# Two attention layers and two feed-forward layers on one core: the SwiGLU output transposed by DMA, expert programs written out, weight rounding in small pieces

## The reference

```python
x = x + attention_1(layernorm(x), ctx)      # 16 heads of 16, softmax
x = x + ffn_1(layernorm(x))                 # SwiGLU, 704 hidden columns, activations and weights rounded to 8 bits
x = x + attention_2(layernorm(x), ctx, ctx) # 4 heads of 64, gated (mLSTM), rms norm
x = x + experts(layernorm(x))               # 8 experts, the best 2 of each row
```

```python
logits = x @ gate_w;  weights, chosen = top_k(softmax(logits), 2);  weights /= weights.sum(-1)
for i in range(8):
    wi = where(chosen == i, weights, 0).sum(-1)
    h  = silu(x @ w1[i]) * (x @ w3[i])          # 256 -> 1024
    out += (h @ w2[i]) * wi
```

## Time and profile before

| | us |
|---|---|
| median of 3 runs | 826.21 (825.64 to 830.43) |
| the profiled execution | 830.6, its span 828.8 |
| attention 1, to the last `tail_add` | about 199 |
| first to last start of a tile's gate/up product, tiles 1 to 38 | 448.42 to 798.48 |
| PE busy | 677.7 (82%) |
| DVE busy | 505.0 (61%) |
| ACT busy | 417.8 (50%) |
| POOL busy | 253.9 (31%) |
| granted TensorE clock, mean | 0.893 |

### The profile page before, as it was taken

The page is one execution under the profiler, slowest core; times in us unless marked ns, Lnnn a source line. Parts: engine busy times, 40 slices in busy tenths (PEclk is TensorE's granted clock), DMA queues, the critical chain, the costliest instruction groups (busy, mean ns, idle before and its releaser), DMA issues.

```text
span 828.8 us, 18605 instructions
## 1 busy us (share of the span) xinstructions
PE 677.7 (82%) x4518; PEld 464.0 (56%) x4519; DVE 505.0 (61%) x1266; ACT 417.8 (50%) x927; POOL 253.9 (31%) x297
## 2 busy tenths in 40 slices
PE   2999999985866686577517999999999999999992
PEld 2788887764324334477413656566656656556661
DVE  5577779987597533688795464646455555464440
ACT  1466665555769335576324544645354545544420
POOL 3111111110245301544302253535344254353211
PEclk9799999997798897755558999999999999999996
DMA  9100000003000002311371525343432534612113
GB/s 271 34 13 13 13 13 13 7 1 102 1 0 0 1 15 108 124 37 32 102 256 27 161 45 132 77 134 76 115 88 34 170 85 124 182 28 32 32 14 114
DMA packets 45649, 58.46 MB, mean 71 GB/s; under 512 B 13296, under 2 KB 39216, under 8 KB 45072
## 3 DMA queue, kind: packets, MB, share of 16 engines
q1 hardware_dynamic: 38128, 47.79, 17.7%
q0 software_dynamic: 7488, 10.31, 7.8%
HBM read 145.90 MB, written 11.80 MB: 190 GB/s over the span
## 4 chain that ended last, share of the span: by engine, by line
PE 46%; DVE 19%; issue 17%; DMA 7%; ACT 3%; POOL 3%; DVEq 2%; ACTq 1%; POOLq 1%; SPq 0%
PE psum L991 14%; PE psum L1013 7%; DMA sum_dram<-region,row_token 5%; PE psum L705 3%; PE psum L689 3%; PE psum L712 3%; PE psum L1004 2%; PE psum L896 2%; PE psum L725 2%; PE psum L744 1%; PE psum L827 1%; PE psum L694 1%; DVE region L1366 1%; PE psum L886 1%; DVE region L1364 1%
## 5 line engine op out<-in xcount | busy, mean ns | idle before, releaser
L991 PE MATMUL psum<-region 128*128 x936 | 216.5, 381 | 15.0 <-issue 5.9
L991 PEld LDWEIGHTS psum<-region 128*128 128x128 bf16 x936 | 91.7, 98 | 116.6 <-issue 27.9
L633 POOL DMA_INDIRECT sum_dram<-region,row_token x39 | 62.1, 1593 | 198.1 <-DVE region L1870 196.0
L1013 PE MATMUL psum<-region 128*128 x936 | 110.2, 275 | 3.4 <-DVE region L1878 3.3
L1269 ACT ACTIVATE region<-psum 128x512 f32<-128x512 f32 x78 | 46.4, 595 | 113.7 <-PE psum L991 113.7
L1013 PEld LDWEIGHTS psum<-region 128*128 128x128 bf16 x936 | 91.5, 99 | 16.1 <-issue 5.1
L1853 DVE TENSOR_TENSOR region<-psum,region 128x512 f32<-128x512 f32 x78 | 54.0, 692 | 64.9 <-ACT region L1269 64.4
L1290 ACT ACTIVATE pause_a<-one_col 128x1 f32<-128x1 f32 x117 | 23.7, 202 | 77.9 <-issue 63.5
L526 POOL TENSOR_TENSOR region<-region,pair_mask 128x256 f32<-128x256 f32 x32 | 18.9, 612 | 137.9 <-ACT region L1058 137.9
L625 POOL DMA_INDIRECT region<-xrow_dram,row_token x39 | 40.9, 1048 | 59.6 <-DVE row_token L1848 27.2
L1878 DVE TENSOR_TENSOR region<-psum,region 128x1024 bf16<-128x1024 f32 x39 | 47.6, 1222 | 14.8 <-ACT region L1277 14.8
(11 more groups left out here) (297 smaller groups left out, 1294.9 us busy)
## 6 DMA issues: line engine op xcount, KB each, us to landing
region<-in_L_ffn_w SPq DMA_DIRECT2D x117, 1024.0 KB
region<-in_ctx SPq DMA_DIRECT2D x32, 128.0 KB, 2.5
region<-neg_max_dram SPq DMA_DIRECT2D x4, 1024.0 KB, 4.7
xrow_dram<-region SPq DMA_DIRECT2D x1, 2080.0 KB, 7.9
x_sb<-in_x SPq DMA_DIRECT2D x4, 512.0 KB, 6.6
region<-in_ctx SPq DMA_DIRECT2D x2, 1024.0 KB, 6.9
sum_dram<-x_sb SPq DMA_DIRECT2D x1, 2048.0 KB, 7.5
region<-in_L_ffn_w_down SPq DMA_DIRECT2D x1, 704.0 KB, 8.3
```

Source lines behind the costliest of these rows:

```text
L633: pool.indirect_dma_start(sum_dram, bass.IndirectOffsetOnAxis(ap=row_token[:, t:t + 1], axis=0), y_d[:, t % 2, :], None, compute_op=ALU.ad ...
L991: last = mm(psum[:, 2 * f + n, :], (xT_lo if xl else xT_hi)[:, p, k, :], weights_at(place, wl, n, k * F1 + f * FH, FH), start=(i == 0), st ...
L1013: last = mm(psum[:, 7, 0:D], (hT_lo if hl else hT_hi)[:, f, :], weights_at(place, wl, 2, f * D, D), start=(i == 0), stop=(i == 3 * (F1 // ...
```

## The change

1. **Expert stage, h.** PE's transposes of h are gone. Each half f of h is split before it is transposed: ACT copies 512 columns of `h_d` to bf16 as soon as the half is there, DVE makes the low half beside it (`h_pair`, 1024 bf16 columns), and SP issues one transposing DMA for each half (`transpose_h`, 128 x 1024 bf16, 256 KB). `down_d` waits for both transfers of its tile.
2. **Expert stage, order.** PE transposes x of tile t + 1 between the two halves of gate/up; ACT's and DVE's x split moves ahead with it. SP's step t is: the two transposing DMAs of tile t, then the loads of w3 for t + 4, w1 for t + 3 and w2 for t + 2.
3. **Programs.** PE's and SP's loops over tiles are written out; PE reads a tile's place once, in the middle of the second half of the tile before.
4. **Attention 1.** DVE's preparation of ffn 1 is cut into small pieces, in steps 2 to 15, and stands ahead of `tail_add` instead of behind it. POOL's and DVE's loops are written out; the power for the layer norm comes in three parts.

```diff
@@ PE, SP: one expert tile
-            def h_transposes(t, p):
-                pe.wait_ge(h_d_ready, 2 * t + 2)
-                for f in range(F1 // P):
-                    last = tr(bank(4, F1 // P, P, count=2)[:, f, :], h_d[:, p, f * P:(f + 1) * P], ident[:])
-                last.then_inc(th_done, 1)
-
-            def down_d(t, place, inner=False):
-                pe.wait_ge(hT_low, t + 1)
+            def down_d(t, place):
+                pe.wait_ge(hT_loaded, 32 * t + 32)
...
+                    half, c = divmod(f, FH // P)
+                    last = mm(psum[:, 7, 0:D], hT_d[:, t % 2, half, hl * (FH // P) + c, :], weights_at(place, wl, 2, f * D, D),
...
-                gate_up_half(t, p, 0, place, inner)
-                if inner or t >= 1:
-                    h_transposes(t - 1, 1 - p)
...
-                gate_up_half(t, p, 1, place, inner)
-                if inner or 0 < t < NT - 1:
-                    x_transposes(t + 1, 1 - p, loads_next, inner)
-                if inner or t >= 1:
-                    down_d(t - 1, place_of(t - 1), inner)
+                gate_up_half(t, p, 0, places[t])
+                if t < NT - 1:
+                    x_transposes(t + 1, 1 - p)
+                gate_up_half(t, p, 1, places[t])
+                if t >= 1:
+                    down_d(t - 1, places[t - 1])
...
+            def transpose_h(t, f):
+
+                sp.wait_ge(h_low_ready, 2 * t + f + 1)
+                if t >= 1 and f == 0:
+                    sp.wait_ge(hT_loaded, 32 * t)
+                if t >= 2 and f == 0:
+                    sp.wait_ge(dn_done, t - 1)
+                sp.dma_start_transpose(hT_d[:, t % 2, f, :, :], h_pair[:, t % 2, f, :]).then_inc(hT_loaded, 16)
...
-                if inner or t + 4 < NT:
-                    load_part(0, t + 4, p, inner)
-                    load_part(1, t + 4, p, inner)
-                if inner or t + 3 < NT:
-                    load_part(2, t + 3, 1 - p, inner)
...
+            for t in range(NT):
+                transpose_h(t, 0)
+                transpose_h(t, 1)
+                if t + 4 < NT:
+                    load_part(1, t + 4)
+                if t + 3 < NT:
+                    load_part(0, t + 3)
+                if t + 2 < NT:
+                    load_part(2, t + 2)
@@ ACT and DVE: one expert tile
-            def h_high(t):
-                act.wait_ge(th_done, t + 1)
-                act_fn(hT_hi, bank(4, F1 // P, P, count=2), ACT.Copy).then_inc(hT_high, 1)
+            def h_high(t, p, f, inner=False):
+                act.wait_ge(h_d_ready, 2 * t + f + 1)
...
+                act_fn(h_pair[:, p, f, 0:FH], h_d[:, p, f * FH:(f + 1) * FH], ACT.Copy).then_inc(h_high_ready, 1)
...
+            def h_low(t, p, f):
+                dve.wait_ge(h_high_ready, 2 * t + f + 1)
+                tt(h_pair[:, p, f, FH:2 * FH], h_d[:, p, f * FH:(f + 1) * FH], h_pair[:, p, f, 0:FH],
+                   ALU.subtract).then_inc(h_low_ready, 1)
@@ DVE: attention 1
-                if late:
-                    late()
+                for work in late:
+                    work()
+                if inner or b >= 1:
+                    tail_add(b - 1)
...
-            rest = (gate_up_maxima, weight_scales, down_rounded, gate_up_scaled, gate_up_shifted, gate_up_rounded, early_norms)
...
+            late[2] = [lambda: gate_up_maxima(0)]
+            late[3] = [lambda: gate_up_maxima(1)]
+            late[4] = [lambda: gate_up_maxima(2)]
+            late[5] = [down_maxima]
+            late[6] = [weight_scales, lambda: down_scaled_up(0)]
+            late[7] = [lambda: down_scaled_up(1), down_shifted]
+            late[8] = [down_rounded, lambda: gate_up_scaled(0, 1)]
+            late[9] = [lambda: gate_up_scaled(1, 5)]
+            late[10] = [lambda: gate_up_scaled(5, 8), lambda: x1_eps(0)]
+            late[11] = [lambda: gate_up_scaled(8, 12)]
+            late[12] = [lambda: gate_up_shifted(0), lambda: early_norms(0, 0, 2)]
+            late[13] = [lambda: gate_up_shifted(1), lambda: early_norms(0, 2, 4)]
+            late[14] = [lambda: x1_eps(1), gate_up_rounded]
+            late[15] = [lambda: early_norms(0, 4, 8), lambda: early_norms(1, B // 2, EARLY)]
```

More of the change, by code:

```diff
@@ L535, in _, with x1_rstd @@
             pool.wait_ge(consts_ready, 7)
[L536 to L540, removed]
-            for n, part in enumerate((slice(0, EARLY), slice(EARLY, B))):
+            def x1_rstd(n):
+                part = THIRDS[n]
                 pool.wait_ge(ln2_eps, n + 1)
                 nc.gpsimd.tensor_tensor(rstd[:, part], rstd[:, part], minus_half[:, part], ALU.pow).then_inc(rstd2_ready, 1)
+            for b in range(B):
+                mask_k(b, b % 2)
+                if b == EARLY:
+                    x1_rstd(0)
+            x1_rstd(1)
+            x1_rstd(2)
             def hidden_product(g, t):
@@ L993, in gate_up_half, with x_transposes @@
                 last.then_inc(gu_done, 1)
-            def x_transposes(t, p, loads, inner=False):
-                pe.wait_ge(xg_loaded[p], 16 * loads)
+            def x_transposes(t, p):
+                pe.wait_ge(xg_loaded[p], 16 * (t // 2) + 16)
                 for k in range(KT):
@@ L1324, in _ @@
             tile_step(NT - 1, 0, (NT - 1) // 2)
-            h_high(NT - 1)
         @block.vector
@@ L1396, in token_stats, with step @@
                 nc.vector.tensor_copy(mv[:, b, :], mv1[:]).then_inc(chain, 1)
-            def step(b, p, inner=False, late=None):
+            def step(b, p, inner=False, late=()):
                 softmax_shift(b, 0)
@@ L1457, in norm_x1, with early_norms @@
                                             ALU.subtract, ALU.mult).then_inc(x1n_step, 1)
-            def early_norms():
-                dve.wait_ge(rstd2_ready, 1)
-                norm_x1(range(EARLY))
+            def early_norms(n, first, end):
+                if first == THIRDS[n].start:
+                    dve.wait_ge(rstd2_ready, n + 1)
+                norm_x1(range(first, end))
             step(0, 0)
-            rest = (gate_up_maxima, weight_scales, down_rounded, gate_up_scaled, gate_up_shifted, gate_up_rounded, early_norms)
-            with dve.Fori(0, (B - 1 - len(rest)) // 2) as i:
-                step(2 * i + 1, 1, inner=True)
-                step(2 * i + 2, 0, inner=True)
-            for b in range(B - len(rest), B):
-                step(b, b % 2, late=rest[b - (B - len(rest))])
+            late = [[] for b in range(B)]
+            late[2] = [lambda: gate_up_maxima(0)]
[12 more added lines that the diff above has]
+            late[15] = [lambda: early_norms(0, 4, 8), lambda: early_norms(1, B // 2, EARLY)]
+            for b in range(1, B):
+                step(b, b % 2, late=late[b])
             tail_norm(B - 1)
@@ L1882, in tile_step @@
                 hidden_d(t, p, 0)
-                if inner or t >= 1:
-                    h_low(t - 1)
-                if not inner and t == 0:
-                    x_low(1, 1)
+                if inner or t < NT - 1:
+                    x_low(t + 1, 1 - p)
+                h_low(t, p, 0)
                 hidden_d(t, p, 1)
-                if inner or 0 < t < NT - 1:
-                    x_low(t + 1, 1 - p)
+                h_low(t, p, 1)
                 if inner or t + 2 < NT:
@@ L1909, in _ @@
             tile_step(NT - 1, 0, NT // 2 + 1)
-            h_low(NT - 1)
             weighted(NT - 1, 0)
```

137 lines of the change are left out of this document (68 added, 69 removed).

## The result

The changed kernel took 902.8 us (median of 4 runs, 902.4 to 903.7) against 827.4 for the one before: a ratio of 1.091, 95% interval 1.087 to 1.095. The forecast was 817, the range 801 to 845.

A forecast was written before the change was run, and what follows sets the result against it. PE's own work was taken to bound the expert stage and attention 1, except where something is late. Terms -35 - 11 + 40 + 4 - 7 = -9 us, from the median 826.2, gave 817 us; range 801 to 845, the forecast's own 806 to 824.

The forecast's parts named there:

- PE's tile, 8.2 us: Steady expert tile: without h's transposes and a second place read it falls from 9.16 to 8.2 us, -35 us in all.
- Together they have some 5 us of work in a tile of 8.2, so only where they stand in a chain matters: Expert stage, ACT and DVE: their copies and subtractions fit within a tile and matter only where a chain waits on them.
- The chain behind a half: End of a tile's second half to transfer issue: silu, product, high, low and issue take 3.1 us, leaving 5.1 for landing.
- The transfers: Transposing DMAs of h: 256 KB land in 3.7 us, within the 5.1 us free, so the sum stays as it is.
- rival 3: Expert stage: transposing DMA lands late, a tile takes (11.3 + L) / 2; at L = 8 us, 846 us; chance 0.20.
- Rival 4: Transposing DMA goes block by block, eight blocks taking 20 us, a tile 40, about 2,000 us in all; chance 0.05.
- A change of expert, 22.1 us: Seven expert changes: chain grows from 19.2 to 22.1 us against 16.4 of PE work; +40 in place of -11.
- The late load: Change of expert: w1, loaded behind a transposing DMA and w3's load, comes 1.5 us late, bounds 0 to 2.5.
- The clock, +4, above 0.95: PE's clock falls at one or two of seven changes, +4 us, bounds 0 and 20; expert-stage granted clock above 0.95.
- the two I had: PE's wait at a change of expert: some 2.5 us before the down product and 3.2 before gate/up.
- Attention 1, -7: Attention 1: DVE's pieces stand where it idles anyway, -7 us, bounds -4 and -10; last `tail_add` at about 191.
- Written-out programs, nothing: Loops written out: costed at nothing, since steady tiles show no idle at loop ends beyond 0.1 us.

The follow-up runs named there:

- e4: Changed kernel with ACT's and DVE's tile loops written out and a tile's place and mark read once: 871.8 us, ratio 1.053.
- e5: Changed kernel with both high halves of h copied on DVE, behind its product, instead of on ACT: 866.7 us, ratio 1.049.
- e3: Changed kernel with the two transposing transfers of a tile replaced by plain ones, leaving the transpose out of the computation: 883.5 us, ratio 1.069.
- e8: e11 with ACT's and DVE's expert programs also written out and table values read once: 831.8 us, ratio 1.003.
- e11: Kernel before with the attention 1 part and PE's and SP's expert programs written out: 811.0 us, ratio 0.976.
- e7: e4 with SP's load of w1 for tile t+3 issued ahead of tile t's transposing transfers: 838.3 us, ratio 1.012.
- e9: e7 with POOL's low half of w1 ahead of its scatter of tile t-1 instead of behind it: 830.9 us, ratio 1.001.
- e17: e9 with the two transposing transfers of a tile replaced by plain ones, leaving the transpose out: 818.4 us, ratio 0.987.
- e1: Kernel before with the change's attention 1 part alone: 821.6 us, ratio 0.992.
- e2: Kernel before with PE's and SP's expert programs written out and a tile's place read once: 821.0 us, ratio 0.989.
- e13: Changed kernel with only w1's load for tile t+3 put ahead of tile t's transposing transfers: 887.1 us, ratio 1.069.
- e15: e8 with POOL's low half of w1 put ahead of its scatter: 811.6 us, ratio 0.978.

## Why the prediction was wrong, step by step

- **PE's tile, 8.2 us:** right as a bound, 8.0 in e4. The changed kernel did not reach it, because of the next step.
- **"Together they have some 5 us of work in a tile of 8.2, so only where they stand in a chain matters":** this is the step that failed. I counted busy time. Table reads are not busy, nor are hand-overs. The chain behind a half, put at 3.1 us, took 6.8, since silu comes 4.1 us after PE's end instead of 0.17. Measured price: 36 us in steady tiles; e4 and e5 give back 31 and 36 (and e3 19: the shares overlap). The page of before had the reads already, in a row that I did not use:

```profile
L1290 ACT ACTIVATE pause_a<-one_col 128x1 f32<-128x1 f32 x117 | 23.7, 202 | 77.9 <-issue 63.5
```

  They cost nothing in a steady tile there, as e8 against e11 shows (8.8 us in both); the change put them into the chain.
- **The transfers:** the transfer was right, 3.3 us for an assumed 3.7, and rival 3, tile = (11.3 + L) / 2, was right in form for a wrong reason: what was late was the issue. Rival 4 is out: eight blocks in 3.3 us. The Trainium skill's "VectorE: DVE Perf Modes", The three transpose paths, has 1309 ns for one block; no run here took one block alone, but eight did not cost eight times that. The Trainium skill's rule that transposing is as fast as plain ("Advanced Engine Details and Errata", X-Bar Transpose (TRN2)) is off here by 0.9 us a transfer, or 12 to 19 us a kernel.
- **A change of expert, 22.1 us:** it took 29.2, which is the larger part of the miss, 50 us. The late load was seen but mis-sized: 1.5 us forecast with 2.5 as the upper bound, 3.3 in the row above and 25.4 us over the seven; issuing w1 earlier gave 16 us alone and 33 after e4. The scatter in front of w1's low half on POOL cost 7 (e7 to e9), and part of the rest is the transfers (12.5, e9 to e17). The hold-up between POOL and DVE was missing altogether; what it cost by itself is not shown. In the kernels where the low half of h reads PSUM it was not touched (1.21 us beside POOL's subtraction in e8, at most 1.23 in before). The Trainium skill's "SBUF — State Buffer", Who interferes with whom, says that a DVE instruction with two inputs in SBUF and a POOL instruction that reads SBUF exclude each other, and the second waits for the whole of the first. The trace agrees: 4.50 us for 0.69 in after, and POOL's pause in e8.
- **The clock, +4, above 0.95:** wrong. 0.86 to 0.95 in the windows and 31 us more of matmul time; PE waited in more places than the two I had. In e9, where it waits less, gate/up and down are busy for 338.5 us instead of 356.4 (before 326.7).
- **Attention 1, -7:** right. The last `tail_add` comes at 191.86 (forecast 191, before 198.37) and e1 measured -7.4 alone.
- **Written-out programs, nothing:** they were worth -8 by themselves (e2); tiles 0 to 38 took 345.5 us for 356.2. I had read only one idle of 0.10 us.

The balance: 902.8 - 31.0 (tables) - 33.5 (w1) - 7.4 (POOL) = 830.9; 12.5 more go with plain transfers, 818.4. That this is near the forecast's 817 is chance: it is a kernel without the transpose and with three mends. The terms depend on their order (e13 against e7), so each holds for this one only. Not settled is how the wait for gathers at the changes, 32 us of PE's in e17 without the first, would go.

## What to carry to other kernels

Two engines with half their time free can still be the bound, if each piece goes back and forth between them and both read tables in between. Count the engine's program from one fixed point to the next, waits and `issue` included, not its busy time. When a step moves from PSUM to SBUF, ask which other engine's long instruction it will now meet. And a load that moves behind two transfers in an in-order queue must be costed as its issue time, its landing, and everything in the program that waits behind it.

## What the hardware showed that I had not expected

- A table read (two registers) left 0.7 to 0.9 us of `issue` in ACT in a steady tile of after, three times a tile. Reading once, with the loops written out, took most steady tiles from some 9.7 to 8.0 us.
- POOL's one-column pause took 2.79 us while DVE ran a subtraction with two SBUF inputs; DVE's 0.69 us low half took 4.50 us behind POOL's 4.04. Both ways the second ended just behind the first, by 0.03 and 0.55 us. The order decides, as e15 and e8 show, which differ by 20 us with the same work. A DVE copy with one input was held up too, 4.58 us for 0.42 in e5.
- A 256 KB transposing transfer within SBUF landed 3.3 us after the low half, a plain one 2.4; of that, issuing it took SP 1.24 us for 0.47. It is many small packets (128,038 in after against 56,902 in e3, for the same 79.22 MB). Behind three 1 MB loads its issue took 4.6 us in e9.
